# Words per address, loaded two halves at a time, in the sum of attention values of a graph network kernel

## The chip, the cores and the metric

The kernel runs on one core of one Trainium2 chip. The metric is the device time of one execution in microseconds, the median of several runs. Engines are named as in the profile: PE is TensorE (PEld its weight loads), DVE is VectorE, ACT is ScalarE, POOL is GpSimd, SP is SyncE. [...]

## What is computed

Four graph layers run one after the other on 6250 nodes and 100000 edges: attention with 8 heads, attention with 4 heads, a four-step graph convolution, and a two-step GIN. Two places matter here. The first is the end of the second layer, which sums weighted values by destination node:

```python
p = jnp.exp(score - m[dst])
denom = jax.ops.segment_sum(p, dst, num_segments=n)
alpha = p / jnp.maximum(denom[dst], 1e-16)
msg = v[src] * alpha[:, :, None]
out = jax.ops.segment_sum(msg, dst, num_segments=n)
```

The second is the GIN, computed with the edge counts as a dense 6272 x 6272 matrix:

```python
agg = jax.ops.segment_sum(x[src], dst, num_segments=x.shape[0])
h = x + agg
h = jax.nn.relu(h @ Wa + ba)
return h @ Wb + bb
```

## The kernel before

**The sum of values** (`sum_values`, L1032). The edges are sorted by destination. 104 pairs of *halves* (208 halves, `2 * TURNS`) each hold four tiles of 128 edges. For a half, SP loads 256 KB of edge values, DVE makes one-hot rows of the destinations (L1178) and multiplies values by weights (L1170), ACT turns the one-hots to float32 (`convert`, L1143), POOL copies the four weights beside the values (L1070), and PE multiplies one-hots by weighted values, four products of 132 columns into PSUM (L1112). Each product adds at a column that depends on the data: the bank and the place of the block of nodes. The blocks fill PSUM's banks in trios, and after every half one bank is carried out by ACT to `m.sums` (`evacuate`, L1150). Whether or not a trio was finished, one bank is evacuated each half; a table says which.

PE brackets an evacuation with two products of zeros (`nought`, L1099): one of 4 columns *closes* the bank and signals ACT (`closed`), one of 396 columns *opens* it again after ACT has read it (`evacuated`). So a half on PE is: close a bank, wait for data, four products, wait for ACT, open the bank.

The columns come from a table in SBUF, made by `places_of_blocks` (L986) on DVE's first partition during the softmax before. Before the change a half has two packed words: each product's column is cut out by shifts and masks (L1108, L1112 register instructions), and the bank likewise (L1103). The words of eight halves, 16 registers, are read by one register load (L1096) at the head of a *turn* of eight halves; the loop of turns is at L1123 (25 rounds, one more turn stands ahead of it). ACT has its own words, eight a turn (L1138).

**The dense layers** (`dense`, L2146). Each of 119 items (7 units of 17) sums three blocks of output nodes over all source blocks in 17 *shares* of three source blocks. In a share, one engine turns a strip of counts into float32 (`moving`: ACT at L2412, DVE at L2557, POOL at L2291; which engine has which share is the string `SHARES = "padpapdpapdapapda"`), and PE multiplies it (L2350). Four `moving` buffers go round, so the strip of share k is made once PE has finished share k-4. Work on a finished item is put between the shares of the next one: `step(g - 1, k)` runs ahead of share k of item g. For GIN items ACT copies the finished sum from PSUM to `d.a` at k = 0 (L2376 to L2378), ahead of its own share 1; PE uses the copy after share 2.

Of the kernel before, what the change touches and what calls it, by code (L numbers as in the profile page):

```python
# [32 lines left out]
HALF = 4  # L33
RINGS = 8
UNROLL = 2 * HALF
TURNS = -(-(TILES + BLOCKS - 1) // UNROLL)
# [10 lines left out]
A1 = D + H1  # L47
SC = COLS * H1
BANKS = 8
TRIOS = -(-BLOCKS // 3)  # L50
TRIO_SUMS = 3 * A1
EVACS = 2 * TURNS + 8
TURN_HALVES = 8
assert 2 * TURNS % TURN_HALVES == 0 and EVACS % TURN_HALVES == 0

F32 = mybir.dt.float32
# [6 lines left out]
ALU = mybir.AluOpType  # L63
ACT = mybir.ActivationFunctionType
AX = mybir.AxisListType
ds = bass.ds
# [330 lines left out]
def wait(engine, sem, n):  # L397

    if not (isinstance(n, int) and n <= 0):
        engine.wait_ge(sem, n)  # L400


def registers(nc, engine, name, n=HALF):
    return [engine.alloc_register(f"{name}{k}") for k in range(n)]
# [581 lines left out]
def places_of_blocks(dve, m, ct, vec):  # L986


    count = 0

    def then(op):
        nonlocal count
        count += 1
        op.then_inc(vec, 1)
        dve.wait_ge(vec, count)

    row = lambda t, size, first=0: t[0:1, first:first + size]
    block_f, bank_f, trio_f, trio_i = row(m.ring4[0], COLS), row(m.ring4[1], COLS), row(m.ring4[2], COLS), row(m.src, COLS)
    whole, one, real = row(m.ring4[3], EVACS), row(m.ring4[3], EVACS, 256), row(m.ring4[3], EVACS, 512)
    moved = row(m.prod, EVACS + 1)  # L1000
    bank_i = row(m.ring4[3], EVACS, 768).bitcast(I32)
    for_pe = ct.tables[0:1, 0:2 * EVACS].rearrange("p (j n) -> p j n", n=2)
    for_act = ct.tables[0:1, 2 * EVACS:3 * EVACS]

    then(dve.tensor_copy(block_f, m.block[0:1, :]))
    then(dve.tensor_scalar(trio_i, m.block[0:1, :], 43.0, None, ALU.mult))
    then(dve.tensor_scalar(trio_i, trio_i, 7, None, ALU.arith_shift_right))
    then(dve.tensor_copy(trio_f, trio_i))
    then(dve.tensor_scalar(trio_i, trio_i, BANKS - 1, None, ALU.bitwise_and))
    then(dve.tensor_copy(bank_f, trio_i))  # L1010
    then(dve.scalar_tensor_tensor(block_f, trio_f, -3.0, block_f, ALU.mult, ALU.add))
    then(dve.tensor_scalar(bank_f, bank_f, 512.0 / 4, None, ALU.mult))
    then(dve.scalar_tensor_tensor(block_f, block_f, A1 / 4, bank_f, ALU.mult, ALU.add))
    then(dve.tensor_copy(whole, trio_f[:, 0:EVACS * HALF:HALF]))
    then(dve.memset(whole[:, 2 * TURNS:EVACS], float(TRIOS)))
    then(dve.memset(one, 1.0))
    then(dve.memset(moved[:, 0:1], 0.0))
    then(dve.tensor_tensor_scan(moved[:, 1:EVACS + 1], one, whole, 0.0, ALU.add, ALU.min))
    then(dve.tensor_tensor(real, moved[:, 1:EVACS + 1], moved[:, 0:EVACS], ALU.subtract))
    then(dve.scalar_tensor_tensor(real, moved[:, 1:EVACS + 1], -float(TRIOS + 1), real, ALU.add, ALU.mult))  # L1020
    then(dve.tensor_scalar(real, real, float(TRIOS), TRIO_SUMS / 4, ALU.add, ALU.mult))
    then(dve.tensor_scalar(bank_i, moved[:, 1:EVACS + 1], float(BANKS - 1), None, ALU.add))
    then(dve.tensor_scalar(bank_i, bank_i, BANKS - 1, None, ALU.bitwise_and))
    then(dve.tensor_copy(whole, bank_i))
    then(dve.scalar_tensor_tensor(for_act, whole, float(1 << 11), real, ALU.mult, ALU.add))
    step = lambda k: block_f[:, k:EVACS * HALF:HALF]
    then(dve.scalar_tensor_tensor(for_pe[:, :, 0], step(1), float(1 << 10), step(0), ALU.mult, ALU.add))
    then(dve.scalar_tensor_tensor(one, step(3), float(1 << 10), step(2), ALU.mult, ALU.add))
    then(dve.scalar_tensor_tensor(for_pe[:, :, 1], whole, float(1 << 20), one, ALU.mult, ALU.add))


def sum_values(nc, m, ct, edge_values):  # L1032
# [3 lines left out]
    with Phase(nc, "va1", "used made hot hit_ready weights_ready weighted evacuated closed betaed skipped parted "  # L1036
# [11 lines left out]
        most = (BANKS - 1) * 512 + 2 * A1  # L1048

        def column(value, last):  # L1050
            return nc.s_assert_within(value, 0, last, skip_runtime_bounds_check_because="places_of_blocks makes no other columns")
# [14 lines left out]
        @block.gpsimd  # L1066
        def _(pool):
            def half(j, r):
                wait(pool, used, j - 3)
                pool.tensor_copy(msg[r][:, :, D:A1],  # L1070
                                 m.weight[:, ds(j * (HALF * H1), HALF * H1)].rearrange("p (k n) -> p k n", n=H1)).then_inc(weights_ready, 1)

            def skip_product(g):
                pool.tensor_tensor(blocks(by_skip[g]), blocks(m.feat[:, g * GN:(g + 1) * GN]), copies(m.beta_of_skip, 1, GB),
                                   ALU.mult).then_inc(skipped, 1)

            wbeta = m.spread["wbeta"]
            for j in range(4):
                half(j, j)
            pool.tensor_tensor(m.beta_of_sum, wbeta[:, 0:D], wbeta[:, 2 * D:3 * D], ALU.add).then_inc(betaed, 1)  # L1080
            pool.tensor_tensor(m.beta_of_skip, wbeta[:, D:2 * D], wbeta[:, 2 * D:3 * D], ALU.subtract).then_inc(betaed, 1)
            pool.wait_ge(betaed, 2)
            for g in range(GROUPS):
                for r in range(4):
                    half(4 * (g + 1) + r, r)
                skip_product(g)
            with pool.Fori(GROUPS + 1, TURNS // 2) as i:
                for r in range(4):
                    half(4 * i + r, r)

        @block.tensor
        def _(pe):
            regs = registers(nc, pe, "va1pe", 2 * TURN_HALVES)

            def load(j):
                pe.load(regs, ct.tables[0:1, ds(j * 2, 2 * TURN_HALVES)])  # L1096

            def nought(at, opens, n=TRIO_SUMS):
                return pe.matmul(m.ps[:, at], nothing[:, 0:P], nothing[:, 0:n], start=opens, stop=not opens)  # L1099

            def half(j, r):
                last = isinstance(j, int) and j >= 2 * TURNS
                low, high = (pe.snap(x, min_val=0, max_val=(1 << 23) - 1) for x in regs[2 * r:2 * r + 2])  # L1103
                done = ds(column((high >> 20) * 512, (BANKS - 1) * 512), TRIO_SUMS)
                nought(ds(column((high >> 20) * 512, (BANKS - 1) * 512), 4), False, 4).then_inc(closed, 1)
                if not last:
                    at = [column(x * 4, most) for x in (low & 1023, low >> 10, high & 1023, (high >> 10) & 1023)]
                    pe.wait_ge(hit_ready, j + 1)  # L1108
                    pe.wait_ge(weights_ready, j + 1)
                    pe.wait_ge(weighted, j + 1)  # L1110
                    for k in range(HALF):
                        mm = pe.matmul(m.ps[:, ds(at[k], A1)], hit[r % 4][:, k, :], msg[r % 4][:, k, :], start=False, stop=False)  # L1112
                    mm.then_inc(used, 1)
                pe.wait_ge(evacuated, j + 1)
                nought(done, True)

            pe.wait_ge(made, 2)
            for k in range(BANKS):
                nought(slice(512 * k, 512 * k + TRIO_SUMS), True)
            load(0)  # L1120
            for j in range(TURN_HALVES):
                half(j, j)
            with pe.Fori(1, 2 * TURNS // TURN_HALVES) as i:  # L1123
                load(TURN_HALVES * i)
                for r in range(TURN_HALVES):
                    half(TURN_HALVES * i + r, r)
            load(2 * TURNS)
            for j in range(2 * TURNS, EVACS):
                half(j, j % TURN_HALVES)
            for k in range(BANKS):  # L1130
                nought(slice(512 * k, 512 * k + 4), False, 4)

        @block.scalar
        def _(act):
            regs = registers(nc, act, "va1act", TURN_HALVES)

            def load(j):
                act.load(regs, ct.tables[0:1, ds(j + 2 * EVACS, TURN_HALVES)])  # L1138

            def convert(j, r):  # L1140
                act.wait_ge(hot, j + 1)
                wait(act, used, j - 3)
                act.activation(hit[r], hit16[:, r].rearrange("p n k -> p k n"), ACT.Copy).then_inc(hit_ready, 1)  # L1143

            def evacuate(j, r):
# [1000 lines left out]
def dense(nc, m, d, t, tables, adj, out):  # L2146
# [14 lines left out]
    with Phase(nc, "de", names) as (  # L2161
# [201 lines left out]
        def _(act):  # L2363
# [5 lines left out]
            def step(g, k):  # L2369
# [3 lines left out]
                if normed(kind) and k == 2:  # L2373
                    act.wait_ge(scaled, upto("scaled", e))
                    act.activation(d.b[:, 0:width], d.a[:, 0:width], ACT.Relu, bias=m.column[f"c{u + 1}"]).then_inc(relued, 1)
                if kind in ("gin", "gin_right") and k == 0:  # L2376
                    act.wait_ge(eaten, (g + 1) * len(SHARES))
                    act.activation(d.a[:, 0:width], y, ACT.Copy).then_inc(copied, 1)  # L2378
                if kind in ("gin", "gin_right") and k == 5:
# [533 lines left out]
```

## Time and profile before

| | us |
|---|---|
| median of 3 runs | 5402.13 |
| lowest and highest | 5399.48, 5411.69 |
| the profiled execution's own time | 5400.67 |
| its span in the trace | 5398.3 |
| its mean granted TensorE clock | 0.885 of 2.4 GHz |
| PE busy, PEld busy | 4350.4, 3655.1 |
| DVE, ACT, POOL busy | 3580.8, 2266.3, 2766.0 |

Busy time is the union of an engine's instructions. The sum of values lies from about 2742 to 3108 us of the span, and the dense layers from about 3210 us to the end, where PE is busy nearly without a break. The time around the span is the profiled execution's time less its span, 2.4 us.

### The profile page before, as it was taken

To read this page: it belongs to the slowest core of one execution; us is meant where nothing else is said; L and a number is where in the kernel's file an instruction comes from. 1 tells how busy PE (TensorE), PEld (TensorE's weight loads), DVE (VectorE), ACT (ScalarE), POOL (GpSimd) and SP (SyncE) were. 2 spreads that over 40 slices of the span, in tenths; PEclk is the share of its full clock that TensorE was granted. 3 is DMA by queue.
4 is the path that set the end of the run, shared out by engine and by line. 5 is a ranking of instruction groups with operands and counts; after the bars stand their busy time and mean duration, and the time that the engine had idled before them with its cause. 6 is when DMAs were issued, how large, how long until landed. Compare 5 with 4: busy or idle time off the path is not lost. (4 is left out here: it accounts for less than half of the span.)

```text
span 5398.3 us, 99723 instructions
## 1 busy us (share of the span) xinstructions
PE 4350.4 (81%) x24072; PEld 3655.1 (68%) x24073; DVE 3580.8 (66%) x7929; ACT 2266.3 (42%) x4134; POOL 2766.0 (51%) x2730
## 2 busy tenths in 40 slices
PE   7566666766767777777468849999999999999998
PEld 4455555554344444444257639999999999999998
DVE  4888888888778888888776674444445654444444
ACT  0333434343245555555246644444444443344333
POOL 0477777774077777777221104444444443344433
PEclk8788888888977787777789959999999999999999
DMA  1444444443267777777235434343444443233332
GB/s 41 124 117 117 118 117 117 116 118 99 96 182 198 200 200 197 203 201 202 70 111 157 136 114 152 132 154 145 149 155 156 174 141 118 96 144 138 133 126 95
DMA packets 543103, 750.01 MB, mean 139 GB/s; under 512 B 57967, under 2 KB 441966, under 8 KB 542734
## 3 DMA queue, kind: packets, MB, share of 16 engines
q1 hardware_dynamic: 461182, 521.35, 28.8%
q0 software_dynamic: 81552, 224.63, 15.5%
q8 instruction: 123, 2.02, 0.1%
q14 instruction: 246, 2.02, 0.1%
HBM read 584.36 MB, written 161.41 MB: 138 GB/s over the span
## 5 line engine op out<-in xcount | busy, mean ns | idle before, releaser
L544 POOL DMA_INDIRECT arena<-table_kv,arena x1664 | 1721.9, 1035 | 653.5 <-issue 506.4
L2350 PE MATMUL ps<-moving,parts 128*128 128x384 f32 (+1 forms) x11662 | 2015.3, 331 | 36.3 <-ACT moving L2412 20.4
L2350 PEld LDWEIGHTS ps<-moving,parts 128*128 128x128 f32 x11662 | 1948.7, 188 | 70.1 <-ACT moving L2412 29.4
L2291 POOL CAST moving<-counts 128x1152 fp32r<-128x1152 uint8 (+1 forms) x420 | 476.7, 1135 | 736.8 <-PE ps L2350 604.7
L340 ACT ACTIVATE counted<-ps 128x392 uint8<-128x392 f32 x1568 | 665.0, 502 | 324.5 <-PE ps L331 283.7
L2291 POOL CAST moving<-big 128x1152 fp32r<-128x1152 uint8 (+1 forms) x413 | 468.4, 1134 | 608.6 <-PE ps L2350 608.6
L331 PE MATMUL ps<-by_place,by_lo 128*128 128x392 bf16 x1568 | 631.3, 525 | 101.9 <-DVE by_place L295 95.5
L654 PE MATMUL ps<-arena 128*128 128x137 f32 x1664 | 325.2, 352 | 338.1 <-DVE arena L788 322.3
L2412 ACT ACTIVATE moving<-counts 128x1152 fp32r<-128x1152 uint8 (+1 forms) x360 | 366.9, 1024 | 436.5 <-PE ps L2350 433.6
L2412 ACT ACTIVATE moving<-big 128x1152 fp32r<-128x1152 uint8 (+1 forms) x354 | 360.4, 1023 | 429.2 <-PE ps L2350 429.0
L654 PEld LDWEIGHTS ps<-arena 128*128 128x128 f32 x1664 | 276.8, 242 | 367.6 <-ACT arena L699 217.6
L2557 DVE CAST moving<-counts 128x1152 fp32r<-128x1152 uint8 (+1 forms) x240 | 312.8, 1303 | 287.2 <-PE ps L2350 287.2
L2557 DVE CAST moving<-big 128x1152 fp32r<-128x1152 uint8 (+1 forms) x236 | 307.5, 1303 | 288.8 <-PE ps L2350 288.8
L562 PEld LDWEIGHTS ps<-arena 128*128 128x128 bf16 x1680 | 141.6, 123 | 523.5 <-DVE arena L556 450.8
L321 DVE TENSOR_TENSOR slots<-slots,counted 128x196 uint16 x1568 | 406.6, 259 | 89.1 <-DVE slots L321 43.0
L562 PE MATMUL ps<-arena 128*128 128x128 bf16 x1680 | 199.6, 252 | 271.5 <-DVE arena L556 269.0
L295 DVE TENSOR_TENSOR by_place<-count_fours,count_place 128x1568 bf16<-128x1568 f16 (+1 forms) x497 | 395.6, 796 | 0.0
L331 PEld LDWEIGHTS ps<-by_place,by_lo 128*128 128x128 bf16 x1568 | 187.7, 123 | 249.2 <-issue 179.2
L883 PE MATMUL ps<-big,arena 128*128 x1672 | 313.5, 348 | 0.4 <-ACT arena L909 0.4
L883 PEld LDWEIGHTS ps<-big,arena 128*128 128x128 f32 x1672 | 292.3, 257 | 27.9 <-issue 18.6
L666 PE MATMUL ps<-big,arena 128*128 x1680 | 288.9, 330 | 0.4 <-ACT arena L694 0.4
L704 ACT ACTIVATE arena<-arena 128x32 f32<-128x32 f32 x208 | 48.3, 232 | 571.5 <-DVE arena L781 571.5
(329 smaller groups left out, 5311.9 us busy)
## 6 DMA issues: line engine op xcount, KB each, us to landing
counts<-adjacency SPq DMA_DIRECT2D x53, 2352.0 KB, 8.6
big<-adjacency SPq DMA_DIRECT2D x52, 2352.0 KB, 8.5
adjacency<-slots SPq DMA_DIRECT2D x784, 98.0 KB
edge_values<-arena SPq DMA_DIRECT2D x208, 256.0 KB, 3.3
arena<-edge_values SPq DMA_DIRECT2D x208, 256.0 KB, 3.2
arena<-table_kv,arena POOLq DMA_INDIRECT x1664
big<-table_norm SPq DMA_DIRECT2D x60, 192.0 KB, 5.6
big<-adjacency SPq DMA_DIRECT2D x7, 1568.0 KB, 6.5
```

The costliest lines, as they stand in the source:

```text
L295: return dve.tensor_tensor(ct.by_place[:, r % 2, n], ct.fours[:, n], copies(ct.place[:, ds(c * HALF, HALF)], 1, last - first), ALU.is_equal)
L321: dve.tensor_tensor(ct.slot_pairs[:, ds(to[k], WIDE // 2)], ct.slot_pairs[:, ds(of[k], WIDE // 2)], ct.counted_pairs[:, r % 2, k, :], ALU. ...
L331: pe.matmul(m.bank(bank, WIDE), ct.by_lo[:, r % 2, :, k], ct.by_place[:, r % 2, :, k], start=True, stop=True).then_inc(ct.product, 1)
L340: act.activation(ct.counted[:, r % 2, k, :], m.bank(bank, WIDE), ACT.Copy).then_inc(ct.moved, 1)
L544: pool.indirect_dma_start(m.ring4[r][:, k * 2 * D:(k + 1) * 2 * D], None, table, bass.IndirectOffsetOnAxis(m.src[:, j * HALF + k:j * HALF ...
L562: mm = pe.matmul(bank[:, k * P:(k + 1) * P], m.hit16[:, r, :, k], m.ident16, start=True, stop=True)
L654: mm = pe.matmul(summed(k), m.hit[:, r % 2, k, :], m.msg[:, r % 2, k, :], start=True, stop=True)
L883: mm = pe.matmul(m.bank(6 + h)[:, k * P:(k + 1) * P], m.hitT[:, h, k, :], m.q[:, ds(at[k] * D, D)], start=True, stop=True)
L2291: pool.tensor_copy(to, of).then_inc(by_pool, 1)
L2350: mm = pe.matmul(m.bank(g % 2, n * P), d.parts[SOURCE[u]][:, s + q, t_, :], moving[:, q * n * P:(q + 1) * n * P], start=(s + q == 0 and t_ ...
L2412: act.activation(to, of, ACT.Copy).then_inc(by_act, 1)
L2557: dve.tensor_copy(to, of).then_inc(by_dve, 1)
```

## The change

Each address gets a word of its own: five words a half (`PE_WORDS`), the four product columns and the bank's first column, ready to use. PE holds two sets of ten registers. One register load fills a set with the words of two halves; it is issued in every even half, behind the closing product, and fills the set for the two halves after the next one. The order within a half is turned: four products, wait for the evacuation of the half before, open that bank, close this half's bank. `weights_ready` is no longer waited for by PE but by ACT ahead of `convert` (and POOL makes one more half of weights for it). `places_of_blocks` writes five words by four copies and one multiplication. And in the dense layers ACT's copy of a finished GIN sum moves from k = 0 to k = 2.

```diff
+PE_WORDS = HALF + 1
...
-    for_pe = ct.tables[0:1, 0:2 * EVACS].rearrange("p (j n) -> p j n", n=2)
-    for_act = ct.tables[0:1, 2 * EVACS:3 * EVACS]
+    for_pe = ct.tables[0:1, 0:PE_WORDS * EVACS].rearrange("p (j n) -> p j n", n=PE_WORDS)
+    for_act = ct.tables[0:1, PE_WORDS * EVACS:(PE_WORDS + 1) * EVACS]
...
-    then(dve.scalar_tensor_tensor(for_pe[:, :, 0], step(1), float(1 << 10), step(0), ALU.mult, ALU.add))
-    then(dve.scalar_tensor_tensor(one, step(3), float(1 << 10), step(2), ALU.mult, ALU.add))
-    then(dve.scalar_tensor_tensor(for_pe[:, :, 1], whole, float(1 << 20), one, ALU.mult, ALU.add))
+    for k in range(HALF):
+        then(dve.tensor_copy(for_pe[:, :, k], step(k)))
+    then(dve.tensor_scalar(for_pe[:, :, HALF], whole, 512.0, None, ALU.mult))
...
+            half(2 * TURNS, 0)
 
         @block.tensor
         def _(pe):
-            regs = registers(nc, pe, "va1pe", 2 * TURN_HALVES)
-
-            def load(j):
-                pe.load(regs, ct.tables[0:1, ds(j * 2, 2 * TURN_HALVES)])
+            sets = [registers(nc, pe, f"va1pe{k}_", 2 * PE_WORDS) for k in range(2)]
+
+            def load(j, q):
+                pe.load(sets[q], ct.tables[0:1, ds(j * PE_WORDS, 2 * PE_WORDS)])
...
-            def half(j, r):
+            def words(r):
+                return sets[r // 2 % 2][r % 2 * PE_WORDS:(r % 2 + 1) * PE_WORDS]
+
+            def closing(r):
+                return pe.snap(words(r)[HALF], min_val=0, max_val=(BANKS - 1) * 512)
+
+            def half(j, r, ahead=True):
                 last = isinstance(j, int) and j >= 2 * TURNS
-                low, high = (pe.snap(x, min_val=0, max_val=(1 << 23) - 1) for x in regs[2 * r:2 * r + 2])
-                done = ds(column((high >> 20) * 512, (BANKS - 1) * 512), TRIO_SUMS)
-                nought(ds(column((high >> 20) * 512, (BANKS - 1) * 512), 4), False, 4).then_inc(closed, 1)
                 if not last:
-                    at = [column(x * 4, most) for x in (low & 1023, low >> 10, high & 1023, (high >> 10) & 1023)]
                     pe.wait_ge(hit_ready, j + 1)
-                    pe.wait_ge(weights_ready, j + 1)
                     pe.wait_ge(weighted, j + 1)
                     for k in range(HALF):
-                        mm = pe.matmul(m.ps[:, ds(at[k], A1)], hit[r % 4][:, k, :], msg[r % 4][:, k, :], start=False, stop=False)
+                        at = pe.snap(words(r)[k], min_val=0, max_val=most)
+                        mm = pe.matmul(m.ps[:, ds(at, A1)], hit[r % 4][:, k, :], msg[r % 4][:, k, :], start=False, stop=False)
                     mm.then_inc(used, 1)
-                pe.wait_ge(evacuated, j + 1)
-                nought(done, True)
+                if not (isinstance(j, int) and j == 0):
+                    pe.wait_ge(evacuated, j)
+                    nought(ds(closing(r - 1), TRIO_SUMS), True)
+                nought(ds(closing(r), 4), False, 4).then_inc(closed, 1)
+                if r % 2 == 0 and ahead:
+                    load(j + 2, (r // 2 + 1) % 2)
...
             with pe.Fori(1, 2 * TURNS // TURN_HALVES) as i:
-                load(TURN_HALVES * i)
                 for r in range(TURN_HALVES):
                     half(TURN_HALVES * i + r, r)
...
                 act.wait_ge(hot, j + 1)
                 wait(act, used, j - 3)
+                act.wait_ge(weights_ready, j + 1)
                 act.activation(hit[r], hit16[:, r].rearrange("p n k -> p k n"), ACT.Copy).then_inc(hit_ready, 1)
...
-                if kind in ("gin", "gin_right") and k == 0:
+                if kind in ("gin", "gin_right") and k == 2:
                     act.wait_ge(eaten, (g + 1) * len(SHARES))
                     act.activation(d.a[:, 0:width], y, ACT.Copy).then_inc(copied, 1)
```

How instructions stand, in the engines' own order (ISA rows are register instructions that form an address; REGISTER_ALU rows are shifts, masks and sums of registers; TENSOR_LOAD reads words of a table from SBUF into registers; a matmul row with 128x132 is one of the four products, 128x396 opens and 128x4 closes a bank).

PE in the sum of values before, at the head of a turn: the opening product of the last turn's eighth half, the loop, the load, the close and the first register instructions of the next half.

```order
L1099 MATMUL ps<-arena 128x396 [waits va1_evacuated]
L1123 UNCONDITIONAL_BRANCH
L1123 ISA
L1096 TENSOR_LOAD count_tables
L1103 ISA
L1099 MATMUL ps<-arena 128x4
L1108 REGISTER_ALU
```

The load stands between an opening and a closing product, once in eight halves.

PE before, the rest of the next half, from the register instruction behind its closing product to its fourth product.

```order
L1108 REGISTER_ALU
L1112 REGISTER_ALU [waits va1_weighted,va1_weights_ready,va1_hit_ready]
L1112 ISA
L1112 MATMUL ps<-arena 128x132
L1112 ISA
L1112 MATMUL ps<-arena 128x132
L1112 REGISTER_ALU
L1112 ISA
L1112 MATMUL ps<-arena 128x132
L1112 REGISTER_ALU x2
L1112 ISA
L1112 MATMUL ps<-arena 128x132
```

With L1103's ISA ahead of the close and the instruction that holds the further waits, a half has eleven register and wait instructions.

PE after the change, in the loop, from behind an even half's closing product to the opening product of the next half.

```order
L1098 ISA
L1098 TENSOR_LOAD count_tables
L1115 ISA [waits va1_weighted,va1_hit_ready]
L1116 MATMUL ps<-arena 128x132
L1115 ISA
L1116 MATMUL ps<-arena 128x132
L1115 ISA
L1116 MATMUL ps<-arena 128x132
L1115 ISA
L1116 MATMUL ps<-arena 128x132
L1107 ISA [waits va1_evacuated]
L1101 MATMUL ps<-arena 128x396
```

The load now stands between a closing product and the four products of the next half, in every second half; a product has one register instruction, and the wait for the evacuation is held by the register instruction ahead of the opening product instead of by the product.

ACT in the dense layers before, round the change from one GIN item to the next (`big` and `counts` are the two count buffers, so the source of `moving` changes where the next item begins).

```order
L2412 ACTIVATE moving<-big 128x1152
L2366 ACTIVATE parts<-dense_cut 128x3x128
L2412 ACTIVATE moving<-big 128x384
L2378 ACTIVATE dense_a<-ps 128x384
L2412 ACTIVATE moving<-counts 128x1152 x2
L2381 ACTIVATE dense_b<-ps,columns 128x384
```

And after the change, the same place.

```order
L2421 ACTIVATE moving<-big 128x1152
L2375 ACTIVATE parts<-dense_cut 128x3x128
L2421 ACTIVATE moving<-big 128x384
L2421 ACTIVATE moving<-counts 128x1152
L2387 ACTIVATE dense_a<-ps 128x384
L2421 ACTIVATE moving<-counts 128x1152
L2390 ACTIVATE dense_b<-ps,columns 128x384
```

The first strip that ACT makes for the next item (share 1) now stands ahead of the copy instead of behind it.

## Rows read from the trace of the kernel before

**Rows 1.** Groups of instructions, 2740 to 3110 us: engine, shapes, count | busy us, mean ns | idle

```profile
L1112 PE MATMUL ps<-arena 128*128 128x132 f32 x1664 | 266.0, 306 | 17.5 <-issue 6.6 <-POOL arena L1070 1.5 <-DVE arena L1170 1.1
...
L1170 DVE TENSOR_TENSOR arena<-arena,big 128x512 f32<-128x512 f32 x208 | 156.9, 754 | 118.4 <-PE ps L1112 113.1 <-DMA arena<-edge_values 4.4
L1143 ACT ACTIVATE arena<-arena 128x512 f32<-128x512 bf16 x209 | 138.8, 664 | 28.5 <-DVE arena L1178 14.4 <-PE ps L1112 14.0
L1150 ACT ACTIVATE big<-ps x216 | 108.0, 500 | 121.2 <-PE ps L1099 119.2 <-issue 2.0
```

**Rows 2.** Timeline of PE in one turn: start us, length us, instruction, [idle before]

```profile
2895.13 1.19 PE L1112 MATMUL ps<-arena 128*128 128x132 f32 x8 [0.29 <-issue]
...
2900.79 1.19 PE L1112 MATMUL ps<-arena 128*128 128x132 f32 x8
2901.82 0.33 PE L1099 MATMUL ps<-arena 128*128 128x396 bf16 x2
2902.12 1.19 PE L1112 MATMUL ps<-arena 128*128 128x132 f32 x8
...
2903.62 1.19 PE L1112 MATMUL ps<-arena 128*128 128x132 f32 x8
...
2907.69 0.18 PE L1099 MATMUL ps<-arena 128*128 128x4 bf16 x1 [1.37 <-issue]
2908.11 1.19 PE L1112 MATMUL ps<-arena 128*128 128x132 f32 x8 [0.25 <-issue]
```

**Rows 3.** The loop's branch, all rounds: ns min/median/max, first and last start us

```profile
L1123 PEldq COMPARE_BRANCH  x25: 76/208/218, 2771.2 to 3095.1; - x25
```

**Rows 4.** Register loads of PE, of 16 and of 4 registers

```profile
L1096 PEldq TENSOR_LOAD <-count_tables x27: 1102/1107/1126, 2742.9 to 3095.2; - x27
...
L393 PEldq TENSOR_LOAD <-arena x419: 327/333/872, 187.8 to 2601.2; - x140
```

**Rows 5.** ACT's register load of 8 and its next instruction, 2905.5 to 2906.4 us

```profile
L1138 ACTq TENSOR_LOAD <-count_tables x1: 546/546/546, 2905.6 to 2905.6; - x1
...
L1141 ACTq ALU_OP  x1: 35/35/35, 2906.2 to 2906.2; - x1
```

**Rows 6.** Timeline of ACT, two evacuations in the turn of rows 2

```profile
2900.97 0.50 ACT L1150 ACTIVATE big<-ps  x1 [0.27 <-PE ps L1099]
...
2902.46 0.50 ACT L1150 ACTIVATE big<-ps  x1 [0.43 <-PE ps L1099]
```

**Rows 7.** PE's register instruction behind the opening product, 2900.9 to 2903.2 us

```profile
L1103 PEldq FUSED_REGOPS  x2: 93/93/93, 2901.5 to 2903.0; - x2
```

**Rows 8.** Timeline of ACT in the last evacuations, which have no products between

```profile
3097.03 0.50 ACT L1150 ACTIVATE big<-ps  x1 [2.11 <-PE ps L1099]
3098.24 0.50 ACT L1150 ACTIVATE big<-ps  x1 [0.71 <-PE ps L1099]
```

**Rows 9.** Stretches: busy us (count) of PE, PEld, DVE, ACT, POOL, then granted clock, DMA

```profile
2921.00:2924.40 3.40, 3.40 (x15) 3.15 (x16) 1.03 (x2) 1.75 (x4) 0.72 (x1) 0.50 0.39 114
...
2900.00:2950.00 50.00, 42.45 (x295) 35.42 (x294) 30.73 (x60) 31.88 (x60) 9.41 (x29) 0.95 0.55 162
```

**Rows 10.** Timeline at the making of the tables, DVE and the next PE work

```profile
2632.77 0.53 DVE L1027 SCALAR_TENSOR_TENSOR count_tables<-arena 1x216 int32<-1x216 f32 x1
...
2635.14 2.05 PE L1220 MATMUL ps<-arena 128*128 128x512 f32 x2 [3.77 <-DVE big L1240]
```

**Rows 11.** Waits of engines from 3110 us: us in total, times, longest

```profile
PE ps L2350 <- ACT moving L2412: 20.4, 35, 0.6
```

**Rows 12.** Timeline of PE, then of ACT, where one GIN item ends and the next begins

```profile
4493.74 2.42 PE L2350 MATMUL ps<-moving,parts 128*128 128x384 f32 x13
4496.75 2.37 PE L2350 MATMUL ps<-moving,parts 128*128 128x384 f32 x12 [0.59 <-ACT moving L2412]
...
4495.15 0.49 ACT L2378 ACTIVATE dense_a<-ps 128x384 f32<-128x384 f32 x1 [2.94 <-PE ps L2350]
4495.54 2.21 ACT L2412 ACTIVATE moving<-big 128x1152 fp32r<-128x1152 uint8 x2
```

More of the change, by code:

```diff
@@ L1011, in places_of_blocks @@
     then(dve.scalar_tensor_tensor(block_f, trio_f, -3.0, block_f, ALU.mult, ALU.add))
-    then(dve.tensor_scalar(bank_f, bank_f, 512.0 / 4, None, ALU.mult))
-    then(dve.scalar_tensor_tensor(block_f, block_f, A1 / 4, bank_f, ALU.mult, ALU.add))
+    then(dve.tensor_scalar(bank_f, bank_f, 512.0, None, ALU.mult))
+    then(dve.scalar_tensor_tensor(block_f, block_f, float(A1), bank_f, ALU.mult, ALU.add))
     then(dve.tensor_copy(whole, trio_f[:, 0:EVACS * HALF:HALF]))
@@ L1119, in _ @@
                 nought(slice(512 * k, 512 * k + TRIO_SUMS), True)
-            load(0)
+            load(0, 0)
             for j in range(TURN_HALVES):
@@ L1123, in _ @@
             with pe.Fori(1, 2 * TURNS // TURN_HALVES) as i:
-                load(TURN_HALVES * i)
                 for r in range(TURN_HALVES):
                     half(TURN_HALVES * i + r, r)
-            load(2 * TURNS)
             for j in range(2 * TURNS, EVACS):
-                half(j, j % TURN_HALVES)
+                half(j, j % TURN_HALVES, j + 2 < EVACS)
+            pe.wait_ge(evacuated, EVACS)
+            nought(ds(closing(EVACS - 1), TRIO_SUMS), True)
             for k in range(BANKS):
@@ L1137, in load @@
             def load(j):
-                act.load(regs, ct.tables[0:1, ds(j + 2 * EVACS, TURN_HALVES)])
+                act.load(regs, ct.tables[0:1, ds(j + PE_WORDS * EVACS, TURN_HALVES)])
             def convert(j, r):
```

## The prediction

> **What bounds the kernel now.** I read first the groups of the sum of values, since most of the edit is there. In one half ACT works about 1.16 us (0.66 convert, 0.50 evacuate), DVE's product 0.75 us with much idle time, and PE's idle time is put down to "issue", hardly to data [rows 1]. So no data is late. The PE timeline then shows the rhythm: from the first product of one half to that of the next 1.33 and 1.50 us by turns, and once in eight halves a hole of 1.37 us ahead of a close [rows 2]. Eight halves take 2908.11 - 2895.13 = 12.98 us; at 1.41 us each they would take 11.3, so the head of a turn costs 1.7 us. The branch rows give the mean turn, (3095.1 - 2771.2) / 24 = 13.50 us [rows 3]; it is longer than the turn shown because in some turns the hole is followed by a stretch at 1.2 GHz: the granted clock is 0.50 in 2921.00:2924.40, and 0.95 on average round it [rows 9].
>
> The hole is the register load: 16 registers take 1.107 us [rows 4], and the engine's sequencer does nothing else meanwhile. ACT shows that a load holds its sequencer even if the next instruction needs none of the loaded words: load at 2905.6 for 0.546 us, a sum of loop registers at 2906.2 [rows 5]. Besides loads, the sequencer is held by waits: PE's instruction behind the opening product starts at 2901.5 and 2903.0, and ACT's evacuations end at 2901.47 and 2902.96 [rows 6, 7]. So the sequencer isn't a queue's length ahead of the array; it comes free when the evacuation ends and then needs its register steps. Eleven of them fill the short interval of 1.33 us: 0.12 us a step with what it issues.
>
> **The dense layers** are simple: 35 times PE waits for a strip made by ACT, 20.4 us in all [rows 11]. At 4495.15 ACT's copy of the finished sum ends its wait for PE; only then does ACT make the strip for share 1, and PE stands for 0.59 us [rows 12].
>
> **The change, part by part.**
>
> *Copy from k = 0 to k = 2.* The strip of share 1 is made while PE still works on the item before (its buffer is free three shares before). The copy still starts when PE has finished the item, takes 0.49 us [rows 12], and PE wants it behind share 2, three shares later; 13 products take 2.42 us [rows 12], a share of six 1.1 us, so it comes over 2 us early. Next late would be ACT's strip for share 4: it may begin when share 1 is done (2.2 us after the item's end), takes 1.1 us (two in 2.21) [rows 12], and is wanted at 4.4: a margin of 1.1 us. The waits belong to the 34 GIN items but for one at the stage's start: 20.4 less 0.6 = **-19.8 us**. Bounds: -17 (the smaller items at a unit's end keep theirs, or some other strip is just late) to -20.4.
>
> *Half without a load ahead (104 of 208).* Its register steps fall from eleven to seven or eight: 0.9 us, no longer the bound; nor are the products, 1.03 us from the first one to the opening product and about 0.17 to the close (0.33 for the pair less the overlap) [rows 2]. What remains is the circle close, evacuate, open, close. Where no products stand between, it takes 3098.24 - 3097.03 = 1.21 us [rows 8]. The change puts one register step, 0.1 us, behind the wait (the address of the opening product). So 1.31 us instead of 1.41.
>
> *Half with a load ahead (104).* The sequencer passes the wait, issues open and close, and only then loads; the array has nothing of the next half yet. From the closing product's start: load begins at 0.1; ten registers at 1.107 / 16 = 0.069 us each take 0.69 [rows 4]; two steps to the first product's weights 0.25; products and opening 1.03, close 0.17; sum 2.24, less 0.02 for register steps no longer between the products: 2.22 us. The evacuation (1.31) is hidden in it, and so is the loop's branch of 0.2 us, since in this half the sequencer isn't held by the wait and gets ahead. Bounds of the load: 0.55 (ACT's eight [rows 5]) and 0.83 (ten at PE's price for four, 0.083 [rows 4]); I take the price per register of the longer PE load, which ACT's eight confirm (0.068). [...]
>
> *Sum of values.* A turn is 4 x 2.22 + 4 x 1.31 = 14.1 us against 13.50: +0.62, times 26 turns **+16 us**. Between the bounds of the load, 104 x -0.14 to 104 x +0.14, that is +1 to +31. The sum says that the turned order and fewer steps win 0.8 us a turn, the vanished big hole 1.7 and the falls of the clock 0.5, and that four loads take 3.6 back. I expect no falls of the clock any more: the longest time without products shrinks from 1.37 to about 0.9 us.
>
> *Small parts.* The extra wait on ACT lies in front of a conversion that has 0.1 to 0.3 us to spare; POOL's extra half and the last evacuations cost nothing that ends last (a load of 0.69 fits beside an evacuation's 1.21). Table making loses three DVE instructions and gets five; they stand on a path on which PE waits 3.77 us for DVE [rows 10]. Five at 0.3 to 0.5 us against three at about 0.5: **+0.5**, bounds 0 to +1.1.
>
> *Sum:* -19.8 + 16 + 0.5 = -3.3. Against the profiled execution's 5400.67 that gives **5397.4 us**; it lies 1.5 us under the median of the runs, 5402.13, so by the median the change would be -0.1%. A measurement of this kernel can tell about 0.2%, 10.8 us, from no change: forecast, no difference.
>
> **Rivals.**
>
> *The loads run beside the products.* If a wait held only the product that carries it, the sequencer would run ahead and loads would be hidden. A pair of halves then needs 16 steps x 0.12 + 0.75 = 2.67 us of sequencer, 1.33 a half, against 13.50 / 8 = 1.69: 208 x -0.36 = -74, with the dense layers -94: about 5307 us. Against it speak rows 6 and 7, and that the wait now stands on a register instruction; for it, that PE's loads of four registers elsewhere (419 of them [rows 4]) lie among products. [...] 13%.
>
> *Slower: the clock falls at the new pauses.* A pause of 0.9 us comes in every pair of halves, four times as often as the hole. In the stretch at 0.50 PE began 15 products in 3.40 us, where 295 in 50 us would be 20 [rows 9]: about 0.9 us lost a fall. With a fall at every second pause that is 52 x 0.9 = 47 us: 5444. It decides from some 16 falls on, which take the time 0.2% over the median. Against it: falls followed pauses of 1.3 us and more, and not all of those. 10%.
>
> *Slower: the dense gap only moves.* If ACT, now held at k = 2, brings share 4 late by as much, 19.8 us don't come: 5417. It decides if a share takes under 0.8 us or ACT's strip over 2 us; the margin of 1.1 us above says no. 6%.
>
> **How the numbers follow.** Forecast 71% with 5385 to 5413 as its own range (the load's bounds and the dense ones); a fifth of it is faster by over 0.2%, a twentieth slower. Faster: 0.71 x 0.2 + 0.13 = 0.27; slower: 0.04 + 0.07 of the clock's case + 0.05 of the dense one = 0.16; within 0.2%: 0.57. The range of 8 in 10, 5377 to 5420, takes in the dense rival and small falls of the clock; it leaves out the hidden loads and many falls.
>
> **What would show it.** In the profile after: PE register loads x107 or so of 0.69 us; the first products of halves alternately 1.3 and 2.2 us apart, with a hole of 0.9 us behind every second close; a turn of 14.1 us; granted clock near 1.0 through the loop; no wait of PE for ACT's strips in GIN items. A turn under 12 us makes the first rival right, clock rows at 0.50 the second, PE waiting at share 4 the third.

## The result and the profile after

| | before | after |
|---|---|---|
| median, us | 5406.91 (4 runs) | 5565.35 (4 runs) |
| lowest and highest | 5399.48, 5413.43 | 5555.17, 5570.58 |
| ratio, 95% interval | | 1.0291 (1.0278 to 1.0304) |
| profiled execution's span | 5398.3 | 5553.4 |
| mean granted TensorE clock | 0.885 | 0.872 |

The change makes the kernel 2.9% slower. I had forecast 5397.4 us and a range to 5420; the result lies far outside. Both kernels' traces, cut at the first and the last product of the sum of values and at the first and the last product of the dense layers, put the 155 us of span where they belong:

| us | before | after | difference | predicted |
|---|---|---|---|---|
| sum of values, first product to last | 348.8 | 529.0 | +180.2 | +16 |
| from there to the dense layers | 125.3 | 129.1 | +3.8 | 0 |
| dense layers, first product to last | 2163.1 | 2136.1 | -27.0 | -19.8 |
| start of the sum of values | 2746.3 | 2743.5 | -2.8 | +0.5 |

The last row says nothing of the change: over the traces of all kernels here that start lies between 2740.9 and 2755.0 us.

**The loads.** The register loads and the loop's branch of after, all of them (ns min/median/max, first and last start in us); they answer to [rows 3, 4]:

```profile
L1098 PEldq TENSOR_LOAD <-count_tables x108: 1072/1750/2435, 2740.0 to 3281.1; - x108
...
L1131 PEldq COMPARE_BRANCH  x25: 76/208/218, 2780.7 to 3272.3; - x25
```

A load of ten words was to take 0.69 us. There are two kinds instead, by turns: 1.08 us and 2.41 us (the median of 1750 ns is the middle of the two). A turn takes (3272.3 - 2780.7) / 24 = 20.48 us against 13.50, and 26 times that difference, 181 us, is the stage's whole growth.

The rows of PEldq hold neither products nor weight loads: in the 24 turns of after's loop they are 96 TENSOR_LOAD, 1272 FUSED_REGOPS and 96 ALU_OP (register arithmetic), 192 EVENT_SEMAPHORE (at the lines that wait) and the branch, 25 times. While one of after's 108 loads runs, no other of them starts, and it is so for PE's loads in this stage of every kernel here. What I call PE's sequencer is what these rows show.

**The rhythm.** The timeline of PE in after, where the eight products of a row are four pairs (start us, length us, [idle before]):

```profile
2979.91 2.12 PE L1116 MATMUL ps<-arena 128*128 128x132 f32 x8 [2.63 <-issue]
...
2982.22 2.11 PE L1116 MATMUL ps<-arena 128*128 128x132 f32 x8
...
2984.92 1.83 PE L1116 MATMUL ps<-arena 128*128 128x132 f32 x8 [0.25 <-issue]
...
2986.78 1.15 PE L1116 MATMUL ps<-arena 128*128 128x132 f32 x8
2987.87 0.34 PE L1101 MATMUL ps<-arena 128*128 128x396 bf16 x2
2990.81 1.16 PE L1116 MATMUL ps<-arena 128*128 128x132 f32 x8 [2.60 <-DVE arena L1179]
...
2992.01 1.15 PE L1116 MATMUL ps<-arena 128*128 128x132 f32 x8
...
2994.70 1.16 PE L1116 MATMUL ps<-arena 128*128 128x132 f32 x8 [1.27 <-issue]
...
2995.90 1.15 PE L1116 MATMUL ps<-arena 128*128 128x132 f32 x8
```

Read the first products from 2986.78 on: 4.03 us to the next half, then 1.20, 2.69, 1.20. These are a half with the long load, one without, one with the short load, one without, all with products at full speed (1.15 us). Two such rounds would be a turn of 18.24 us. Above them stand halves whose eight products take 2.12 us: half the clock, after a hole of 2.63 us. The releaser "DVE arena L1179" at 2990.81 misleads. The load in that hole is this one:

```profile
L1098 PEldq TENSOR_LOAD <-count_tables x1: 2414/2414/2414, 2988.1 to 2988.1; - x1
```

It ends at 2990.5, and DVE's product (row of DVE's timeline below) had ended at 2990.2:

```profile
2989.52 0.68 DVE L1179 TENSOR_TENSOR arena<-arena,big 128x512 f32<-128x512 f32 x1
```

**The clock.** Stretches of after; the columns are those of [rows 9], the granted clock stands third from the end:

```profile
2979.90:2984.10 4.20, 4.20 (x18) 3.91 (x19) 0.91 (x2) 1.05 (x2) 0.20 (x1) 0.50 0.21 62
2990.80:2996.00 5.20, 3.92 (x31) 3.48 (x32) 2.15 (x4) 2.12 (x4) 0.40 (x2) 1.00 0.34 101
...
2800.00:3050.00 250.00, 163.51 (x980) 141.60 (x980) 108.07 (x196) 103.74 (x198) 27.68 (x100) 0.84 0.35 103
```

The slow halves run at 0.50, the others at 1.00; over the loop the clock is 0.84, where it was 0.95. No row gives it in GHz; what stands above as 1.2 and 2.4 GHz is 0.50 and 1.00 of the granted clock. In after's trace the product behind an opening one of 396 columns starts mostly 167 or 168 ns after it at 1.00 and 331 or 332 ns after it at 0.50, which is 2.4 columns a nanosecond and 1.2. Nearly every long hole is followed by a fall: of 48 holes over 2 us in the trace's loop 45 are, the one at 2979.91 for instance; the one at 2990.81 is among the three that aren't. What a turn takes above 18.24 us I put down to the falls: 20.48 - 18.24 = 2.2 us.

**The dense layers.** PE's waits for ACT's strips, in after (us in total, times, longest), against [rows 11]:

```profile
PE ps L2359 <- ACT moving L2421: 1.1, 2, 0.6
```

And ACT's timeline in after where one GIN item ends, against [rows 12]:

```profile
4673.40 1.17 ACT L2421 ACTIVATE moving<-big 128x1152 fp32r<-128x1152 uint8 x1 [1.56 <-PE ps L2359]
4674.79 0.49 ACT L2387 ACTIVATE dense_a<-ps 128x384 f32<-128x384 f32 x1 [0.21 <-PE ps L2359]
4675.83 1.17 ACT L2421 ACTIVATE moving<-big 128x1152 fp32r<-128x1152 uint8 x1 [0.55 <-PE ps L2359]
```

The strip now stands ahead of the copy, and ACT has idle time before the strip behind it (0.55 us): the gap is gone and moved nowhere. But the gain is 27.0 us and not 19.8. The same waits in before, told of the weight loads' row instead of the products', had the right size:

```profile
PEld ps L2350 <- ACT moving L2412: 29.4, 34, 0.9
```

From one copy of a finished sum to the next, a GIN item took 21.76 us in before (4451.63 to 4473.39) and takes 20.87 us in after (4612.17 to 4633.04): 0.89 us less.

### The profile page after: what moved, and what is told of

Same layout as the page of the kernel before. It is cut to its first block and busy times, and to the rows that moved or that the text cites. A ratio compares the mean times of both kernels' runs of the same rounds, so it can differ in the third digit from the quotient of the medians.

```text
span 5553.4 us, 99220 instructions
## 1 busy us (share of the span) xinstructions
PE 4400.1 (79%) x24072; PEld 3716.3 (67%) x24073; DVE 3586.6 (65%) x7931; ACT 2269.8 (41%) x4134; POOL 2748.5 (49%) x2731
## 5 line engine op out<-in xcount | busy, mean ns | idle before, releaser
L655 PEld LDWEIGHTS ps<-arena 128*128 128x128 f32 x1664 | 281.2, 246 | 361.4 <-ACT arena L700 214.5
L1116 PE MATMUL ps<-arena 128*128 128x132 f32 x1664 | 311.9, 343 | 182.2 <-DVE arena L1179 105.1
L1116 PEld LDWEIGHTS ps<-arena 128*128 128x128 f32 x1664 | 270.0, 243 | 218.4 <-issue 216.2
L1071 POOL COPY arena<-big 128x16 f32 (+1 forms) x209 | 52.2, 250 | 594.3 <-PE ps L1116 457.3
L884 PE MATMUL ps<-big,arena 128*128 x1672 | 319.7, 353 | 0.4 <-ACT arena L910 0.4
```

Of the source, the lines that this page charges most:

```text
L655: mm = pe.matmul(summed(k), m.hit[:, r % 2, k, :], m.msg[:, r % 2, k, :], start=True, stop=True)
L1116: mm = pe.matmul(m.ps[:, ds(at, A1)], hit[r % 4][:, k, :], msg[r % 4][:, k, :], start=False, stop=False)
```

## The experiments

What was open: why a load of ten words takes 1.08 us or 2.41, if its price explains the whole stage, if the turned order does what I said, and if the dense part stands by itself. The theory, from the loads in both traces (4 words 0.33, 16 words 1.11 in [rows 4], ACT's 8 words 0.55 in [rows 5]): a load reads in steps of about 0.24 us; if it starts on a multiple of 16 bytes, a step brings four words, and what is left over comes one word a step; if not, every step brings one word. This is a theory, to be tried below. Pairs of halves start 40 bytes apart in the changed kernel, so every second one starts 8 bytes off. Rivals: the loads of one of the two register sets are slow; or loads are slow when other engines use SBUF.

**A price list (p1_loads).** In the kernel before, loads of several lengths and starts, put ahead of the loop, four of each kind.

```diff
+            for _ in range(4): pe.load(regs[0:4], ct.tables[0:1, 0:4])
+            for _ in range(4): pe.load(regs[0:4], ct.tables[0:1, 1:5])
...
+            for _ in range(4): pe.load(regs[0:16], ct.tables[0:1, 2:18])
```

> The kernel before, with 64 extra register loads on PE ahead of the first half of the sum of values, four of each kind (words, first word): 1, 2, 4, 8, 10, 12 and 16 words from offsets of 0, 1, 2 or 4 words; nothing uses them. Theory (groups of four): a load that starts on a multiple of 16 bytes reads four words at a time, what is left over, and every word of a load that starts elsewhere, one at a time; each such read about 0.24 us, 0.09 us for the whole. So 4 words at 0: 0.33; 8 at 0 or 4: 0.57; 16 at 0 or 4: 1.05; 12 at 0: 0.81; 10 at 0: 1.05; 2 at 0: 0.57; 4 at 1 or 2: 1.05; 8 at 2: 2.0; 10 at 1 or 2: 2.4; 12 at 2: 3.0; 16 at 2: 3.9 us. Rival (second set of registers): offsets change nothing, 10 words take about 1.08 from any. Rival (traffic: loads are slow because they lie among products): all of these, ahead of any product, stay near 0.07 us a word, 10 words 0.69.

The trace has none of the added loads, only the 27 of before; nothing uses their results, and I take that as the reason. 5394.74 us, in effect one run of the kernel before. It tells nothing; the price has to be measured on loads that the kernel needs.

**Ten words at a step of twelve (e1_stride12).** Each pair's ten words start every 48 bytes, always on a multiple of 16; two words lie unused between.

```diff
+STRIDE = 6
...
-                pe.load(sets[q], ct.tables[0:1, ds(j * PE_WORDS, 2 * PE_WORDS)])
+                pe.load(sets[q], ct.tables[0:1, ds(j * STRIDE, 2 * PE_WORDS)])
...
```

> The changed kernel with the ten words of a pair of halves at a stride of twelve words, so that every load starts on a multiple of 16 bytes; still ten registers. Groups of four: every load 1.08 us, none of 2.4; a turn at 15.6 us if the clock holds, the sum of values 100 to 125 us shorter than in the changed kernel, 5440 to 5470 us. Second set of registers: loads alternate 1.08 and 2.4 us as before and the time stays near 5565. Traffic: loads keep a mean of 1.75 us, no gain.

The loads and the branch of this kernel, then its granted clock over the loop, then one pause in PE's timeline:

```profile
L1099 PEldq TENSOR_LOAD <-count_tables x108: 1072/1081/1095, 2743.1 to 3160.2; - x108
...
L1132 PEldq COMPARE_BRANCH  x25: 76/208/218, 2777.6 to 3152.7; - x25
```

```profile
2800.00:3050.00 250.00, 168.65 (x1280) 144.17 (x1280) 138.15 (x257) 134.98 (x257) 27.79 (x129) 1.00 0.46 135
```

```profile
2882.38 1.16 PE L1117 MATMUL ps<-arena 128*128 128x132 f32 x8 [1.29 <-DVE arena L1180]
```

All loads are short though the two sets still alternate, so it isn't the set; the engines' traffic is denser than in after (DMA share 0.46 against 0.35), so it isn't that either. A turn takes 15.63 us. PE pauses 1.3 us at most, and the clock stays at 1.00. The sum of values is 122.7 us shorter than in the changed kernel, as expected; the time, 5433.92 us, came out 6 us under the range. Ratio 1.006 (1.0044 to 1.0077): still slower than before.

**Ten words at a step of thirteen (e5_stride13).** The four loads of a turn start 0, 4, 8 and 12 bytes behind a multiple of 16.

```diff
+STRIDE = 13
...
-                pe.load(sets[q], ct.tables[0:1, ds(j * PE_WORDS, 2 * PE_WORDS)])
+                pe.load(sets[q], ct.tables[0:1, ds((j * STRIDE) >> 1 if not isinstance(j, int) else j * STRIDE // 2, 2 * PE_WORDS)])
...
```

> Ten words a load as in the change, but a pair of halves starts every 13 words, so that the four loads of a turn start 0, 4, 8 and 12 bytes behind a multiple of 16. Groups of four, only from an aligned start: one load of 1.08 us and three of 2.41 us in every four; at full clock a turn of 15.6 + 3 x 1.33 = 19.6 us, and since two such loads a turn cost 2.2 us more by the falling clock, with three about 22.9 us; time 5540 (no falls) to 5630. Rival 1 (single words up to the next multiple of 16, then groups): at 12 bytes 1.08 us, at 4 bytes about 1.8 us; against the 2.41 us of 8 bytes it has nothing to say. Rival 2 (the slow loads belong to the one of the two register sets): durations alternate by set, two of four slow, whatever the start; a turn of 20.5 us, time 5565.

The loads of one turn, and the clock:

```profile
L1099 PEldq TENSOR_LOAD <-count_tables x4: 1089/2404/2409, 2844.2 to 2860.3; - x4
```

```profile
2800.00:3050.00 250.00, 165.02 (x932) 141.46 (x932) 101.94 (x185) 97.61 (x186) 27.11 (x95) 0.79 0.33 98
```

One of four is short, the aligned one, through the whole loop; 4, 8 and 12 bytes off all cost 2.40 us. That fells both rivals on record. The time, 5591.3 us (one run), is within the range; the turn came out at 21.7 us, less than 22.9: the falls cost 2.1 us a turn with three long loads, as with two, so they don't simply count with them.

**Twelve words (e2_twelve).** A half gets six words, one of them unused, and the load reads all twelve.

```diff
-PE_WORDS = HALF + 1
+PE_WORDS = HALF + 2
```

> The changed kernel with six words a half, the sixth unused: twelve registers a load, always on a multiple of 16 bytes. Groups of four: three reads, 0.81 us, so a longer load is faster than ten words' 1.08; a turn at 14.5 us; 5395 to 5425 us. A price for each word: twelve words take 1.2 to 1.3 times as long as ten do in the run with the stride of twelve words, and this kernel is slower than that one.

```profile
L1098 PEldq TENSOR_LOAD <-count_tables x108: 845/851/865, 2743.4 to 3136.4; - x108
...
L1131 PEldq COMPARE_BRANCH  x25: 83/215/230, 2776.1 to 3129.2; - x25
```

Two words more, and each load is 0.23 us shorter than e1_stride12's: by the theory three steps of four words against two of four and two of one. A price for each word is out. A turn takes 14.71 us. 5408.29 us, within the range; ratio 1.0018 (1.0008 to 1.0027).

**The dense copy alone (e3_dense_only).** The kernel before, with nothing changed but the copy's place.

```diff
-                if kind in ("gin", "gin_right") and k == 0:
+                if kind in ("gin", "gin_right") and k == 2:
```

> The kernel before with only the copy of the GIN sums moved from k = 0 to k = 2. By the comparison of the two traces each of 32 item boundaries is 0.89 us shorter: 27 to 28 us less, 5378 us. By the wait row alone, on which the prediction rested, 20 us less: 5386. If the shorter dense stage came from something in the sum of values (another phase of the clock): no difference.

5373.51 us against 5399.96 on the same chip, ratio 0.9954 (0.9937 to 0.9971): -26.5 us. PE's waits for ACT's strips fall as in after:

```profile
PE ps L2350 <- ACT moving L2412: 1.1, 2, 0.6
```

So this half of the change is worth 0.5%, and the sum of values takes it back more than six times over.

**Load behind the products (e4_behind_products).** Twelve words again, the load moved from behind the close to ahead of the wait for the evacuation.

```diff
+                if r % 2 and ahead:
+                    load(j + 1, (r // 2 + 1) % 2)
                 if not (isinstance(j, int) and j == 0):
...
-                if r % 2 == 0 and ahead:
-                    load(j + 2, (r // 2 + 1) % 2)
```

> Twelve words at 16-byte steps as in e2_twelve, and the load issued behind the fourth product of odd halves, ahead of the wait for the evacuation, instead of behind the closing product. Theory (groups of four; a load holds the sequencer for its length, whatever the array does): the load still takes 0.85 us, but from the issue of the fourth product on the array still has about half a microsecond of products queued and the evacuation takes until 1.3 us after the close, so about 0.5 us of each load is left in view: two halves 3.1 to 3.2 us, a turn 12.6 us against 14.71 in e2_twelve and 13.50 before; time 5350, range 5340 to 5362. Rival (what costs is a load's presence in every pair of halves, not where it stands, because the sequencer drains the array first): a turn stays at 14.7, time as e2_twelve, 5405. Granted clock 1.00 by both.

5396.8 us, ratio 0.9994 (0.9985 to 1.0003): between theory and rival, nearer to the rival. The branch of this kernel, (3125.3 - 2783.5) / 24 = 14.24 us a turn:

```profile
L1131 PEldq COMPARE_BRANCH  x25: 76/208/217, 2783.5 to 3125.3; - x25
```

Its timeline of PE over two halves:

```profile
2899.83 1.16 PE L1116 MATMUL ps<-arena 128*128 128x132 f32 x8 [0.43 <-ACT arena L1152]
2901.36 0.34 PE L1101 MATMUL ps<-arena 128*128 128x396 bf16 x2 [0.37 <-issue]
2901.80 1.16 PE L1116 MATMUL ps<-arena 128*128 128x132 f32 x8
...
2903.21 1.16 PE L1116 MATMUL ps<-arena 128*128 128x132 f32 x8
```

And the conversion by ACT for the half at 2903.21:

```profile
2902.41 0.66 ACT L1152 ACTIVATE arena<-arena 128x512 f32<-128x512 bf16 x1
```

From close to close, away from a turn's head, the half with the load did get shorter, from 2.38 to 1.93 us. But the half without it grew from 1.29 to 1.45: ACT converts for it behind its evacuation, until 2903.07, and PE starts right behind that. And the two halves round a turn's head are together 0.7 us longer than the others, which in e2_twelve they are not. In one turn's head of e2_twelve, ACT's conversion behind its own register load ends at 2896.44, beside PE's load (2895.56 to 2896.41), and PE's loop branch runs at 2893.75 while products are still queued. Here that conversion ends at 2899.69 with no load of PE's beside it, PE's products follow at 2899.83, and the branch stands behind the close. So the cover that the load had given to other work went with it, and of 2.1 us expected 0.5 came.

**The old load at the turn's end (e7_load_at_turns_end).** The kernel before with the dense copy at k = 2, and its one load of 16 words a turn moved likewise.

```diff
                     mm.then_inc(used, 1)
+                    if r == TURN_HALVES - 1:
+                        load(j + 1)
                 pe.wait_ge(evacuated, j + 1)
...
             with pe.Fori(1, 2 * TURNS // TURN_HALVES) as i:
-                load(TURN_HALVES * i)
                 for r in range(TURN_HALVES):
...
```

> The kernel before with the dense copy at k = 2 (as e3_dense_only), and its one load of 16 registers a turn moved from the head of the turn to behind the fourth product of the turn's last half, ahead of the wait for the evacuation; packed words, order in a half and everything else as before. Theory (a load holds only the sequencer, so it costs what is left of it when the evacuation and the products still queued are done): the load stays 1.11 us, of which about 0.5 lie beside the last products and the evacuation; the half with the load falls from 2.84 us to about 2.4, and with no hole of 1.37 us left the clock stays at 1.00, so the slow halves behind it (1.94 and 1.62 us on average in the kernel before) fall to 1.4 to 1.5: a turn 12.3 us against 13.49, range 11.9 to 12.9; over 26 turns 31 us less than e3_dense_only, time 5342, range 5330 to 5358. Rival (the place doesn't matter, since the array drains before the load either way; as seen in e4_behind_products, the cover is lost elsewhere): a turn stays at 13.3 to 13.5, time 5370 to 5374.

5371.07 us against 5392.76, ratio 0.9957 (0.9943 to 0.997): the dense copy's gain and no more. The half with the load takes 2.84 us as before, the mean turn 13.4. Its timeline of PE round the load:

```profile
2900.35 1.24 PE L1112 MATMUL ps<-arena 128*128 128x132 f32 x8
2902.39 0.34 PE L1099 MATMUL ps<-arena 128*128 128x396 bf16 x1 [0.80 <-issue]
2903.03 0.17 PE L1099 MATMUL ps<-arena 128*128 128x4 bf16 x1 [0.30 <-issue]
2903.50 2.08 PE L1112 MATMUL ps<-arena 128*128 128x132 f32 x8 [0.30 <-issue]
```

The holes of 1.37 and 0.25 us [rows 2] are now three, of 0.80, 0.30 and 0.30. Idle time counts from modelled ends, and the half from close to close is no shorter. The evacuation that the load was to lie beside, and the load:

```profile
2900.73 0.50 ACT L1150 ACTIVATE big<-ps  x1 [0.44 <-PE ps L1099]
```

```profile
L1096 PEldq TENSOR_LOAD <-count_tables x1: 1107/1107/1107, 2901.2 to 2901.2; - x1
```

The evacuation ends at 2901.23, and the load starts at 2901.23. It is so in all 25 rounds: the evacuation ends between 0.17 us before and 0.02 us after the load's start. So the sequencer has no wait there beside which a load could lie, and steps, load and branch follow one another in either order. My expectation took the time of the evacuation for free time of the sequencer; here it isn't.

The other part of that expectation failed as well. The longest pause is now 0.84 us, and the clock still falls, eight times in the loop; it is 0.96 against 0.95 before and 0.97 in e3_dense_only:

```profile
2800.00:3050.00 250.00, 217.96 (x1504) 180.72 (x1504) 155.63 (x299) 160.86 (x300) 49.59 (x150) 0.96 0.54 157
```

## Why the prediction was wrong

Mean times of the loop over 24 turns, close to close (halves with and without a load), and the granted clock from 2800 to 3050 us:

| kernel | load, us | half without | half with | turn | clock | stage |
|---|---|---|---|---|---|---|
| before | 1.11, one a turn | | | 13.49 | 0.95 | 348.8 |
| predicted for after | 0.69 | 1.31 | 2.22 | 14.1 | near 1.0 | 365 |
| e2_twelve | 0.85 | 1.30 | 2.38 | 14.71 | 1.00 | 382.6 |
| e1_stride12 | 1.08 | 1.30 | 2.61 | 15.62 | 1.00 | 406.3 |
| after | 1.08 and 2.41 | 1.49 | 2.32 and 4.90 | 20.40 | 0.84 | 529.0 |

**The step that failed is "ten registers at 1.107 / 16 = 0.069 us each take 0.69", with its bounds of 0.55 and 0.83.** I took the price per register of the longer load for a price by the word. The ten registers took 1.08 us and 2.41 us by turns. Shown by e1_stride12 and e5_stride13: the price depends on where the load starts. Shown by e2_twelve beside e1_stride12: it doesn't grow with every word, twelve cost less than ten. All rows that I priced from were loads of 4, 8 or 16 words at multiples of four words in their tables; the table of five words a half breaks both conditions. That a step is 0.24 us and brings four words or one is a fit to six prices, within 0.08 us of each, and not seen itself. Divided by ten, the runs have 0.24 us a register from an unaligned start and 0.11 from an aligned one, where I had put 0.069.

**The half with a load** was right but for that term: 2.22 less 0.69 is 1.53, and 2.38 - 0.85 and 2.61 - 1.08 give 1.53 as well. The load is in full view in its half, as "the sequencer passes the wait, issues open and close, and only then loads" says. **The half without a load** was 1.31 and is 1.30. With the right price these give 4 x 1.30 + 2 x (1.53 + 1.08) + 2 x (1.53 + 2.41) = 18.3 us, which is the 18.24 read from the rows at full clock: (18.24 - 14.1) x 26 = 108 us of the miss.

**"I expect no falls of the clock any more"** hung on that term too: it rested on a longest pause of about 0.9 us. In e1_stride12, where the pauses are 1.3 us at most, the granted clock is 1.00 through the loop and even the falls of before are gone; in after, with pauses of 2.6 us, it falls again and again, 2.24 x 26 = 58 us more. So the rival of the falling clock came true, but at pauses of another length than I had priced, and beside a larger loss. The reason that I gave for no falls, a shorter longest pause, is not borne out either: with pauses up to 1.3 us in every second half there was none in e1_stride12, and with none over 0.84 us there were eight in e7_load_at_turns_end. 108 + 58 and the 16 predicted are 182 us, the 181 of the stage.

**The dense term** had the right mechanism and no moved gap (its rival is out), but was sized at -19.8, with -20.4 as its bound, where -26.5 (alone) and -27.0 (in after) came. I read the idle time of the products, which counts from the modelled end of the last product; the items at whose borders PE waited became 0.89 us shorter, not 0.59. The row of the weight loads, 0.86 us a time, was the one to read.

**Loads beside the products** (the first rival, 5307 us) is out: in e1_stride12 and e2_twelve a half with a load takes 1.53 us and the load's whole length. [rows 6, 7] stand for more than two cases, too: of the 189 register instructions like those of [rows 7] in the loop of before, none starts ahead of the evacuation's end, and 126 start 0.05 us behind it. **Small parts:** making the tables cost 0.4 us, 0.5 said. "A load of 0.69 fits beside an evacuation's 1.21" fell with the price: the stretch from the last product to the dense layers, in which the last evacuations lie, is 3.8 us longer.

**What beats both kernels** is the kernel before with the dense copy at k = 2 alone: 0.9954. No form of the new load tried here did better; with e4_behind_products the whole change comes to no difference.

## What to carry to other kernels

The price of a register load on PE from SBUF wasn't by the word here (ten words 1.08 or 2.40 us by their start, twelve 0.85): start each load on a multiple of 16 bytes, try a length padded to a multiple of four, and before you price a load from rows, ask if its start and length are like theirs. None of the places tried here hid a load: a turn took 14.24 us against 14.71 in e4_behind_products, 13.4 against 13.49 in e7_load_at_turns_end. Ask whether the engine's sequencer would else be waiting at the place that a load is moved to, and not whether the array has work left. And size a wait by the distance between equal starts, for the idle time of a product counts from an end that is modelled: it gave 0.59 us an item here, where the starts gave 0.89.

## What the runs showed of the hardware

- Register loads on PE from SBUF, by their medians: 0.33 us for 4 words; from a multiple of 16 bytes, counted from the start of the table, 0.85 for 12 words, 1.11 for 16 and 1.08 for ten; ten words 2.40 to 2.41 from 4, 8 or 12 bytes off. A longer load can be the faster one. In other stages a load of 4 words took up to 0.87 us [rows 4]; why, no run here shows.
- The granted clock was 1.00 through 250 us in which PE stood still for about 1.3 us in every second half (e1_stride12), where in the kernel before, with one hole of 1.37 us a turn, it was 0.95. With holes of 2.6 us it was 0.84, and three in 48 of these weren't followed by a fall. With no pause over 0.84 us it was 0.96 (e7_load_at_turns_end). So the length of the longest pause doesn't order these kernels; what decides stays open, it wasn't tried by itself.
